# Four edits to a two-block mixture-of-experts kernel: the second block's up-bias on ScalarE, up-projections in two banks, set-ups on VectorE, first block's row copies on ScalarE

## The reference, cut to what matters

```python
# block 0's experts (top 2 of 8, weights from a softmax over the two)
g = jnp.einsum('td,edf->tef', xt, Wg)
u = jnp.einsum('td,edf->tef', xt, Wu)
h = jax.nn.silu(g) * u
y = jnp.einsum('tef,efd->ted', h, Wd)
# block 0's mixer: k, v, r projections, a scan over time, then
out = jnp.einsum('bsd,ed->bse', r * wkv, Wo)
# block 1's experts (L1_ffn): a hidden router layer, top 2 of 8, and per expert
#   silu(x @ we1[e] + be1[e]) @ we2[e] + be2[e]
# block 1's mixer: retention with 16 heads of 8, group norm, gate, projection
```

## Time and profile before

| | us |
|---|---|
| median of 3 runs | 915.49 (913.84 to 917.21) |
| profiled execution, its own time | 917.44 |
| its span, first to last instruction | 915.6 |
| TensorE's mean granted clock in it | 0.869 |

### The profile page before, as it was taken

The page is one execution under the profiler, slowest core; times in us unless marked ns, Lnnn a source line. Parts: engine busy times, 40 slices in busy tenths (PEclk is TensorE's granted clock), DMA queues, the critical chain, the costliest instruction groups (busy, mean ns, idle before and its releaser), DMA issues.

```text
span 915.6 us, 15283 instructions
## 1 busy us (share of the span) xinstructions
PE 691.8 (76%) x5116; PEld 590.2 (64%) x5116; DVE 423.0 (46%) x1286; ACT 362.4 (40%) x683; POOL 432.4 (47%) x459
## 2 busy tenths in 40 slices
PE   2488866874687866795878778999739998967683
PEld 2378864674566866684877777656626658866573
DVE  5642235877497613461133213357773576501102
ACT  1244432872386533451332334443424333532231
POOL 2774656553447355535334645621337343354432
PEclk9999897988789887995777988999959999987777
DMA  8812121013102112201211121100211001113202
GB/s 308 324 45 35 41 84 29 19 27 94 36 19 38 41 41 84 61 22 37 72 44 36 42 75 41 25 7 8 87 17 35 11 24 21 44 40 92 44 24 87
DMA packets 42601, 51.77 MB, mean 57 GB/s; under 512 B 7840, under 2 KB 33696, under 8 KB 42400
## 3 DMA queue, kind: packets, MB, share of 16 engines
q0 software_dynamic: 11776, 24.14, 10.7%
q1 hardware_dynamic: 30752, 26.66, 8.9%
HBM read 33.47 MB, written 17.30 MB: 55 GB/s over the span
## 4 chain that ended last, share of the span: by engine, by line
PE 57%; issue 11%; another core or an unknown queue 11%; DVE 10%; ACT 5%; POOL 2%; DMA 2%; SPq 0%; ACTq 0%; DVEq 0%; POOLq 0%
PE bank L545 23%; PE bank L560 13%; PE bank L650 4%; PE bank L547 2%; PE bank L525 2%; PE bank L672 2%; POOL xs L1073 1%; PE bank L628 1%; DVE hT L1288 1%; PE bank L497 1%; ACT hT L841 1%; PE bank L476 1%; ACT w_up L823 1%; DMA xs<-rows_in,take_from 1%
## 5 line engine op out<-in xcount | busy, mean ns | idle before, releaser
L545 PE MATMUL bank<-xT_kept,w_up 128*128 128x128 f32 x1840 | 320.9, 316 | 110.1 <-issue 42.6
L545 PEld LDWEIGHTS bank<-xT_kept,w_up 128*128 128x128 f32 x1840 | 279.0, 215 | 136.5 <-issue 80.9
L1087 POOL DMA_INDIRECT rows_out<-ys,send_to x184 | 187.3, 1018 | 217.4 <-DVE ys L1299 173.5
L1073 POOL DMA_INDIRECT xs<-rows_in,take_from x184 | 181.4, 986 | 170.4 <-PE bank L525 69.9
L560 PE MATMUL bank<-w,hT 128*128 x1288 | 203.8, 304 | 24.1 <-DVE ys L1299 12.2
L560 PEld LDWEIGHTS bank<-w,hT 128*128 128x128 f32 x1288 | 181.0, 215 | 34.2 <-issue 32.6
L823 ACT ACTIVATE w_up<-w 128x728 f32 (+1 forms) x184 | 131.5, 717 | 76.0 <-PE bank L545 29.8
L1299 DVE COPY ys<-bank 128x256 f32<-128x256 f32 x96 | 39.4, 410 | 200.7 <-PE bank L563 104.3
L841 ACT ACTIVATE hT<-bank 128x512 f32<-128x512 f32 x92 | 54.9, 596 | 182.5 <-PE bank L547 103.1
L1288 DVE TENSOR_TENSOR hT<-gate,bank 128x384 f32<-128x384 f32 x92 | 50.7, 551 | 131.3 <-PE bank L545 45.0
L547 PE MATMUL bank<-bconst,bparts 128*128 x368 | 86.1, 234 | 0.0
(11 more groups left out here) (159 smaller groups left out, 748.0 us busy)
## 6 DMA issues: line engine op xcount, KB each, us to landing
yg<-rows_out SPq DMA_DIRECT2D x64, 128.0 KB
w<-in_w SPq DMA_DIRECT2D x8, 536.0 KB, 10.4
rows_in<-xn SPq DMA_DIRECT2D x16, 256.0 KB
w<-in_w SPq DMA_DIRECT2D x8, 512.0 KB
xs<-rows_in,take_from POOLq DMA_INDIRECT x184
rows_out<-ys,send_to POOLq DMA_INDIRECT x184
x<-in_x SPq DMA_DIRECT2D x2, 512.0 KB, 5.6
decay<-in_decay SPq DMA_DIRECT2D x1, 1024.0 KB
```

What stands on the lines that cost most here:

```text
L545: last = mm(to, w_up[:, n % 2, start_col:start_col + P], rows_in, start=True, stop=(k == 0))
L1073: pool.indirect_dma_start(xs[:, q % 2, t, :], None, xn_dram[b], own).then_inc(ld_xs[q % 2][t], 16)
L1087: pool.indirect_dma_start(y_dram[b], own, ys[:, m % 4 // 2, m % 2 * 2 + j % 2, :], None)\
```

## The change

1. **Up-bias of block 1.** The bias matmul per chunk is gone. The up biases are loaded as eight rows (`up_bias`); the router finds which expert owns each of 24 tiles as a one-hot (`hot`), PE multiplies the two once per pass in 4 small matmuls beside the router's last ones, and DVE copies the result (`tile_bias`). Silu is then 4 instructions of 128 columns, each with the bias of its tile and chunk as a column.
2. **Banks.** In block 0 the second up part goes to bank 1 and bank 4 by turns, so it waits for `h_done` of tile n-2. In passes 4 and 7 (TWO_BANKS) the up-projection goes to banks 0 and 1 by turns, with the same wait; passes 5 and 6, where retention uses bank 1, keep one bank.
3. **Set-ups.** The bias's split (now 128 columns wide, for the down bias alone) and the mixer's set-up are on DVE; POOL keeps two instructions of them.
4. **Row copies.** In block 0 the copies of ys are on ACT, behind the silu of each even tile; in block 1 they stay on DVE.
5. Some small tiles share memory (`slot` is `so_far`; `lg`, `mine` and `ended` are one), and TURNS is new for PE, ACT, POOL and DVE.

```diff
+TWO_BANKS = (4, 7)
...
-        "b12 a2 c10 a c a42 c a50 b7 a b4 a3 b a8 b a3 b a10 b2 a14 b2 a b7 a6 b a2 b a8 c2 a c8 a2 c3 a4 c a14 "
+        "b12 a2 c10 a2 c a20 c a80 b8 a b a b a b3 a3 b a10 b a5 b a9 b9 a7 b a2 b a8 c8 a c3 a2 c2 a9 c a12 c "
...
+        def up_bank(p, j, part=0):
+            n = p * TILES + j
+            if KIND[PASSES[p][0]] == 0:
+                return (1, 4)[n % 2] if part else 0
+            return n % 2 if p in TWO_BANKS else 0
...
+                if k == 1:
+                    if (f, b) == (3, 0):
+                        pe.wait_ge(ld_up_bias, 16)
+                    after(TB_DVE[b], CALL[f], "hot")
+                    for c in range(CH[1]):
+                        last = mm(to[:, 192 + c * NSB:192 + (c + 1) * NSB], up_bias[0:E, c * P:(c + 1) * P], hot[0:E, :],
+                                  start=True, stop=True)
...
-                    if k == 0 and part == 0 and n:
-                        pe.wait_ge(gate_ready, n)
-                    elif n:
+                    own = up_bank(p, j, part)
+                    if k == 0 and part == 0:
+                        if n:
+                            pe.wait_ge(gate_ready, n)
+                    elif k == 0 or j and p in TWO_BANKS:
+                        if n >= 2:
+                            pe.wait_ge(h_done, n - 1)
+                    else:
                         pe.wait_ge(h_done, n)
...
-                        last = mm(to, w_up[:, n % 2, start_col:start_col + P], rows_in, start=True, stop=(k == 0))
-                        if k == 1:
-                            last = mm(to, bparts[:, c * P:(c + 1) * P], bconst[:, bass.ds(e * P + B_SEL, P)],
-                                      start=False, stop=True)
+                        last = mm(to, w_up[:, n % 2, start_col:start_col + P], rows_in, start=True, stop=True)
...
-                    nc.scalar.activation(hT[:, n % 2, :], bank[0][:], ACT.Silu).then_inc(h_done, 1)
+                    if j == 0:
+                        after(TB_DVE[PASSES[p][1]], CALL[PASSES[p][0]], "bias")
+                    for c in range(CH[1]):
+                        own = tile_bias[:, PASSES[p][1], c, j:j + 1]
+                        last = nc.scalar.activation(hT[:, n % 2, c * P:(c + 1) * P], bank[up_bank(p, j)][:, c * P:(c + 1) * P],
+                                                    ACT.Silu, bias=own)
+                    last.then_inc(h_done, 1)
+
+            def copy_y(p, m):
+                n = min(2, TILES - 2 * m)
+                act.wait_ge(down_done, p * TILES + 2 * m + n)
+                if m >= 4:
+                    act.wait_ge(y_sent[m % 4], y_sent_by(p, m - 4))
+                elif p:
+                    act.wait_ge(y_sent[m], y_sent_by(p - 1, NPAIR - 4 + m))
+                nc.scalar.activation(ys[:, m % 4 // 2, m % 2 * 2:m % 2 * 2 + n, :], heads(ybank[:, 0:n * P], n, P), ACT.Copy).then_inc(y_copied, 1)
...
+                if k == 1:
+                    V.tensor_scalar(hot[:], owner[:], 1.0, count[:, P:P + 1], ALU.add, ALU.is_equal).then_inc(TB_DVE[b].sem, 1)
...
+                if k == 1:
+                    V.tensor_copy(tile_bias[:, b, :, :], heads(own[:, 192:192 + CH[1] * NSB], CH[1], NSB)).then_inc(TB_DVE[b].sem, 1)
```

More of the change, by code:

```diff
@@ L159, in build_block @@
         btri = sb("btri", [P, P], BF16)
[L160 removed]
+        bparts = sb("bparts", [P, P], BF16)
+        up_bias = sb("up_bias", [P, F1])
+        tile_bias = sb("tile_bias", [P, NB, CH[1], NSB])
         gn = sb("gn", [P, 2 * P])
@@ L293, in build_block @@
         RT_PE = [Steps(sem(f"route{b}_pe"), ["logits", "count", "inv"]) for b in range(NB)]
+        TB_DVE = [Steps(sem(f"tile_bias{b}_dve"), ["hot", "bias"]) for b in range(NB)]
         RT_ACT = [Steps(sem(f"route{b}_act"), ["tanh"]) for b in range(NB)]
@@ L562, in project_down @@
                 if k == 1:
-                    last = mm(y, bconst[:, bass.ds(e * P + B_SEL, P)], bparts[:, F1:NBIAS], start=False, stop=True)
+                    last = mm(y, bconst[:, bass.ds(e * P + B_SEL, P)], bparts[:, :], start=False, stop=True)
                 last.then_inc(down_done, 1)
@@ L863, in experts @@
                             copy_x(p * NG + j // GRP + 1)
+                        if k == 0 and j % 2 == 0 and (j or p > p0):
+                            yield
+                            copy_y(*((p, j // 2 - 1) if j else (p - 1, NPAIR - 1)))
+                    if k == 0 and p in DRAINED:
+                        yield
+                        copy_y(p, NPAIR - 1)
             def rwkv(b):
@@ L1001, in bias_setup @@
                 step(nc.gpsimd.tensor_tensor(btri[:], bconst[:, B_TRI:B_TRI + P], bconst[:, B_ONE:B_ONE + P], ALU.subtract))
-                yield
-                pool.wait_ge(ld_const, 16 * 2)
-                pool.wait_ge(ld_bias, 16)
-                last = "btri"
-                for i in range(3):
-                    after(SETUP, 0, last)
-                    step(nc.gpsimd.tensor_copy(bias_part, bias_raw))
-                    yield
-                    after(SETUP, 0, f"p{i + 1}")
-                    if i < 2:
-                        step(nc.gpsimd.tensor_tensor(bias_raw, bias_raw, bias_part, ALU.subtract))
-                        yield
-                        after(SETUP, 0, f"r{i + 1}")
-                    own = const[:, K_PART + i:K_PART + i + 1]
-                    if i == 0:
-                        step(nc.gpsimd.tensor_scalar(bparts[:], bias_part, own, None, ALU.mult))
-                    else:
-                        step(nc.gpsimd.tensor_scalar(bias_part, bias_part, own, None, ALU.mult))
-                        yield
-                        after(SETUP, 0, f"m{i + 1}")
-                        step(nc.gpsimd.tensor_tensor(bparts[:], bparts[:], bias_part, ALU.add))
-                    yield
-                    last = f"b{i + 1}"
@@ L1299, in copy_y, with bias_setup, step @@
                 V.tensor_copy(ys[:, m % 4 // 2, m % 2 * 2:m % 2 * 2 + n, :], heads(ybank[:, 0:n * P], n, P)).then_inc(y_copied, 1)
+            def bias_setup():
+                def step(ins):
+                    ins.then_inc(BIAS.sem, 1)
+                yield
+                dve.wait_ge(ld_const, 16 * 2)
+                dve.wait_ge(ld_bias, 16)
+                for i in range(3):
+                    if i:
+                        after(BIAS, 0, f"b{i}")
+                    step(V.tensor_copy(bias_part, bias_raw))
+                    yield
+                    after(BIAS, 0, f"p{i + 1}")
+                    if i < 2:
+                        step(V.tensor_tensor(bias_raw, bias_raw, bias_part, ALU.subtract))
+                        yield
+                        after(BIAS, 0, f"r{i + 1}")
+                    own = const[:, K_PART + i:K_PART + i + 1]
+                    if i == 0:
+                        step(V.tensor_scalar(bparts[:], bias_part, own, None, ALU.mult))
+                    else:
+                        step(V.tensor_scalar(bias_part, bias_part, own, None, ALU.mult))
+                        yield
+                        after(BIAS, 0, f"m{i + 1}")
+                        step(V.tensor_tensor(bparts[:], bparts[:], bias_part, ALU.add))
+                    yield
@@ new lines, in rwkv_setup, with step @@
+            def rwkv_setup():
+                def step(ins):
+                    ins.then_inc(RW_SET.sem, 1)
+                yield
+                dve.wait_ge(ld_const, 16 * 2)
+                dve.wait_ge(ld_sq, 16)
+                for j in range(3):
+                    step(V.tensor_scalar(rw_v[:, j:j + 1], colv[:, MIX + j:MIX + j + 1], -1.0, 1.0, ALU.mult, ALU.add))
+                after(RW_SET, 0, "omm2")
+                for j in range(3):
+                    w = sq[:, M_MIX + j * P:M_MIX + (j + 1) * P]
+                    yield
+                    step(V.tensor_scalar(rw_w[:, 2 * j, :], w, colv[:, MIX + j:MIX + j + 1], None, ALU.mult))
+                    yield
+                    step(V.tensor_scalar(rw_w[:, 2 * j + 1, :], w, rw_v[:, j:j + 1], None, ALU.mult))
+                after(RW_EXP, 0, "exp")
+                step(V.tensor_scalar(rw_v[:, 4:5], rw_v[:, 3:4], -1.0, None, ALU.mult))
+                for buf, value in ((rw_pp, -1e30), (rw_aa, 0.0), (rw_bb, 0.0)):
+                    step(V.memset(buf[:, 0:1], value))
+                after(RW_SET, 0, "bb0")
```

64 lines of the change are left out of this document (25 added, 39 removed), and 37 rows, old and new, of the table TURNS.

## The result

The changed kernel takes 901.69 us (median of 4 runs, 899.38 to 906.17) where the kernel before takes 914.91 beside it: a ratio of 0.9858, 95% interval 0.9814 to 0.9902, so 9 to 17 us faster and 13 by the medians. Forecast were 28. The ratios leave out executions in which the chip was in its slower state, so they need not be the exact quotient of the medians beside them. The profiled execution took 900.73 us, with a span of 898.6.

The account below looks back on a forecast made before the run. PE was taken as the bound in undisturbed tiles, apart from pauses. Up-bias -24, table +1.5, set-ups -2.5, block 0 banks -3 and copies 0 made -28; 917.44 - 28 - 1.95 gave 887 us, range 873 to 902 (8 in 10: 864 to 911).

Parts of the forecast that it names:

- the price of silu: Block 1 on ACT: four silus end 0.54 us later than one, hidden except in about 20 lone one-bank tiles.
- the up-bias term: Block 1: dropping 368 bias matmuls, net of longer silu, saves 43 us, of which -24 us stays.
- the lone tile: Passes 5 and 6, one bank, no other work: 0.89 + 1.29 = 2.18 us, a gain of 0.15 each.
- The bias matmuls' gross worth: PE, block 1's up-projection: a tile's four bias matmuls cost 0.45 us at full clock, 0.85 at half.
- Two banks: Passes 4 and 7: PE doesn't wait for silu, a tile takes 1.88 us, 46 tiles gain 28 us.
- Set-ups: Start of the kernel: with set-ups off POOL the first gather starts earlier, 0 to -2.9 us, taken as -2.5.
- Banks in block 0: Block 0: bank 4 lets PE run one up part ahead of DVE's product, 0 to -7 us, taken as -3.
- Row copies: Block 0: 48 copies of 0.4 us move from DVE to ACT, between -8 and +12 us, taken as 0.
- slower, by ScalarE in block 0: Rival, chance 0.09: tiles beside RWKV, where copies on ACT wait for scatters and delay w_up and silu, 924 us.
- Slower, by the clock: Rival, chance 0.05: PE, with less work per tile, stays at 1.2 GHz through passes 4 and 7, 924 us.
- More comes through: Rival, chance 0.20: pauses stay as long, all 43 us of PE time go, 859 us in all.
- Given back: Rival, chance 0.11: pauses and retention's DVE steps take all the up-bias gain, 911 to 915 us.

Follow-up runs that it names:

- e3: Changed kernel with block 1's silu as one instruction of 512 columns and its up-bias left out: 883.5 us, 0.9625 of the kernel before.
- e9: Changed kernel with all gathers and scatters plain, and block 1's silu as one instruction without its bias: 711.86 us, 0.7903 of the kernel before.
- e8: Changed kernel with every indirect gather and scatter as a plain transfer of as many rows: 718.75 us, 0.7982 of the kernel before.
- e2: Changed kernel with one bank for the up-projections in passes 4 and 7 too: 908.27 us, 0.9898 of the kernel before.
- e1: Changed kernel with the queues of PE, ACT, DVE and POOL in the order of the kernel before: 899.99 us, 0.9811 of the kernel before.
- e7: Changed kernel with block 0's row copies back on DVE: 897.97 us, 0.9973 of the kernel before.
- e4: Changed kernel with a bias matmul again behind each chunk of block 1's up-projection and silu as one instruction: 918.56 us, 1.0029 of the kernel before.
- e12: Changed kernel with its scatters alone as plain transfers, gathers still indirect: 784.54 us, 0.8721 of the kernel before.
- e10: Changed kernel with all gathers and scatters plain, bias matmuls back in block 1's up-projection and silu as one instruction: 748.88 us, 0.8315 of the kernel before.

## Why the forecast was wrong, point by point

The direction and the range (864 to 911) held; the size was half. Of the signs named, the tile of 1.9 us, the four silus and the first gather came; PE's busy time fell by 32 and not by 86 us, and silu's wait without a releaser was 43.5 and not some 70.

Of the 15 us that are missing, the up-bias has 8 (16 ± 6 where 24 were forecast) and all the rest of the change 7 (+3 ± 5 where -4 was forecast).

- **The step that failed is the price of silu in the up-bias term.** The forecast said that PE doesn't wait for the longer silu with two banks, that beside retention other matmuls fill the wait, and that only some 20 lone tiles pay 0.3 us: 6 us. It measured 21 ± 6 (e3). The working took ACT's 1.22 us of idle time in *undisturbed* tiles for its slack everywhere. Without indirect transfers that is about right (7 us, e9 against e8); with them the silu's 0.54 us are paid 21 / 92 = 0.23 us per tile on average. The next point explains at most 20 x 0.27 = 5 us of the 15 that are too few. Which waits in the trace hold the rest isn't shown; that it goes with the indirect transfers is, as far as 14 ± 8 us can show it.
- **Inside the lone tile** a pace stood where a latency belongs. I let the next up-projection start 1.29 us behind silu's release. That came out at 1.28 (790.71 to 791.99), though by luck in its parts: 0.1 to start, 1.14 and 0.05 were added, and it is 1.15 of silu and a gap of 0.14. But I added 0.89 us for the up-projection, which is the *pace* of its matmuls where others stand behind them. Silu waits for the last one to be through, 789.54 to 790.71, 1.17 us, and the tile comes to 1.17 + 1.28 = 2.45 instead of 2.18 us: worse than the 2.33 with the bias matmul. Such tiles were fewer than the forecast's 20: from silu to silu took 2.4 to 2.6 us 10 times in passes 5 and 6 (20 times in e8).
- **The bias matmuls' gross worth** was a quarter too high. Forecast 43 net of silu, so 49 with it; measured 37 ± 6, alike with and without pauses (37 ± 4). That is what PE's busy time says (39 us between e3 and e4). So "a little over half is given back" was a wrong reason, and it hid the silu's price: the pauses take nothing of the matmuls' 37 us. Of -24 us, -16 ± 6 came.
- **Two banks.** Their 46 tiles were the largest part of it, 28 us before giving back; with one bank the forecast's 0.15 per tile would have made 7, so the second bank itself stood for 21. It measured 4 ± 5 us (e2). The pace per tile was right, 1.9 us; the number of tiles that run at it was not: of the 44 intervals from silu to silu within passes 4 and 7, 15 are under 2.1 us (31 in e8). The prediction called PE the bound of such a tile and did not set POOL's 2 x 1.25 = 2.5 us beside it.
- **Table:** forecast +1.5. No run takes it apart.
- **Set-ups.** The first gather did start where forecast, at 32.02 us instead of 35.11:

```profile
32.02 1.21 POOL L1074 DMA_INDIRECT xs<-rows_in,take_from  x1 [21.36 <-DVE cw L1279]
```

  But the first up-projection came only 1.7 us earlier (43.0 instead of 44.7), and pass 0 then took 78.2 us instead of 72.3, with e1's order too (78.4). Nothing is left of -2.5. Ahead of the change set-ups stood between POOL's first 6, next 5 and later gathers; in the changed kernel, and in e1, 12 follow one another without a break, and the chain of pass 0 has 23% without a releaser where it had 5%. That points at the longer run of gathers. No run puts something between them again.
- **Banks in block 0:** forecast -3; with the old order passes 1 to 3 gained nothing (319.8 against 317.5) from banks and copies together. Alone they weren't tested. Whether the new order could have been had without bank 4 wasn't tried.
- **Row copies:** forecast 0, measured -10 ± 5 (e7), outside the lower bound of -8 by its middle. The duration was right (381 ns, forecast 0.4 us). The rival "slower, by ScalarE in block 0" fell with it.
- **The order of the queues was not priced at all.** The text ahead of the prediction showed POOL's 13 gathers in a row at the start, and the prediction made nothing of it. It is one of the largest items here, some 25 us either way: -23 in the first half, +27 in the second, and only their cancelling left the sum alone (+4 ± 6). Which steps of the order do it, and on which queue, isn't shown.
- **What doesn't close.** Everything but the first edit is +3 ± 5 us (e4). Of that the order is +4 and the copies -10, which leaves some +9 ± 9, for set-ups, table and bank 4, where the forecast had -4. Pass 0's 6 us point there, as said above.
- **The rivals.** "Slower, by the clock": the granted clock rose in passes 4 and 7, 0.81 and 0.82 against 0.78 and 0.81. "More comes through" fell on the silus, though its premise, that pauses take nothing back, held for the matmuls. "Given back" fell too: e4 shows the first edit's 16 us.
- **The pauses.** Forecast "the same wait without releaser, some 70 us" for silu. The waits of the changed kernel (us in all, times, longest):

```profile
DVE ys L1304 <- remote: 81.1, 11, 16.0
...
ACT hT L872 <- PE bank L575: 71.6, 46, 6.2
...
ACT hT L872 <- remote: 43.5, 11, 8.5
```

  Silu's fell from 72.9 to 43.5. DVE's copy of ys has one of 16.0 us, beside the piece of 15.94 us in the chain above; the most of it is time in which pass 7 had no down-projection to copy yet. The share of the chain without a releaser went from 11 to 12%.

## What to carry to other kernels

Where one engine waits for another, add what the work takes until it is through, not its pace in a full queue (here 1.17 against 0.89 us). Slack that is read from the quiet tiles of a kernel need not be there in the others: price a longer latency on the path by what all tiles would pay, and take the quiet ones as the lower bound. When a change brings a new order of the queues with it, price the order as an edit of its own, half by half, since two large effects can hide in a small sum; here taking the better half of each gave 0.9564 where the whole orders gave 0.9858 and 0.9811. And set the time of every queue per tile side by side, idle steps included: POOL looked free at 46% busy, yet two transfers a tile took it longer than PE's tile.

## What the runs showed of the hardware

- 368 indirect transfers, of 971 and 1019 ns, made plain (540 and 543 ns) at the same 42616 packets and 51.49 MB took 170 us off POOL's busy time and as much, 19%, off the kernel, though POOL was busy only 46% of the span. While indirect ones follow one another 1.25 us apart, the chain has pieces without any releaser, and silu, a copy and a down-projection that were due stood still together for over 3 us (811.20 to 814.67). So they do behind a run of gathers when only the scatters are plain (717.06 to 720.21, e12). With both plain such pieces are gone from the chain. What in the chip causes them no run shows.
- The granted clock went with it: 0.875 with indirect transfers, 0.925 with plain gathers, 0.908 with plain scatters, 0.936 with both plain.
- 368 matmuls of the bias are worth 37 us, 0.10 us each, with indirect transfers and with plain ones (e4 against e3, e10 against e9), though their rows in the profile read 234 ns each.
- Four activations of 128 columns with a column as bias take 1.14 us here, 372 ns each and spaced so that they overlap, as four of ScalarE's copies did before the change.
